# Local attention and feed-forward of a two-batch transformer: weights, tables and first rows loaded one stage earlier, shifted rows taken from transposed tokens

## What is computed

```python
def shift_token(t):               # second half of the channels from the token before
    t1, t2 = jnp.split(t, 2, axis=-1)
    t2 = jnp.pad(t2, ((0, 0), (1, 0), (0, 0)))[:, :-1]
    return jnp.concatenate([t1, t2], axis=-1)

def _layer(x, wqkv, qs, ksc, wo, lg, lb, w1, b1, w2, b2):
    q, k, v = jnp.split(shift_token(x) @ wqkv, 3, axis=-1)        # to 8 heads of 64
    q = l2norm(q) * qs
    k = l2norm(k) * ksc
    q, k = rotary_xpos(q, k)
    o = local_attention(q, k, v)  # windows of 128 tokens, each sees itself and the one before
    x = x + o @ wo
    h = shift_token(x)
    h = (h - mean(h)) / sqrt(var(h) + 1e-5) * lg + lb
    a, g = jnp.split(h @ w1 + b1, 2, axis=-1)                     # 2 x 682
    return x + (a * gelu(g)) @ w2 + b2
```

## Time and profile before

| | |
|---|---|
| median of 3 runs | 4666.85 us (4664.31 to 4668.85) |
| profiled execution, its own time | 4673.75 us |
| its span | 4672.1 us, mean granted TensorE clock 0.912 |
| TensorE / VectorE / ScalarE / GpSimd busy | 3969.5 / 2966.2 / 2041.8 / 670.3 us |
| output projection of the second attention, batch 0 | 1295.95 to 1321.80 |
| keeping the input | from 1322.99 |
| local attention, layer 0, batch 0 | from 1325.65 |
| feed-forward, layer 0, batch 0 | 1656.07 to 1827.97 |
| local attention, layer 1, batch 0 | from 1829.93 |

### The profile page before, as it was taken

How to read it: one execution, slowest core, us unless ns; L and a number is a source line. 1 busy time by engine, 2 the same in 40 slices (tenths; PEclk the granted TensorE clock), 3 DMA queues, 4 the chain that set the end, 5 groups by cost and what they waited for, 6 DMA issues and landing times. The chain is left out here.

```text
span 4672.1 us, 62196 instructions
## 1 busy us (share of the span) xinstructions
PE 3969.5 (85%) x21496; PEld 1945.2 (42%) x21588; DVE 2966.2 (63%) x5901; ACT 2041.8 (44%) x3649; POOL 670.3 (14%) x526
## 2 busy tenths in 40 slices
PE   7889967989969967996959899589899798779967
PEld 5233344333345534553533333433334354445534
DVE  3878765978657722773269786768785676237623
ACT  2356632456635511553124566215566454125521
POOL 2000004000023201331130000130000222023211
PEclk8799988899989988998978999789999899889989
DMA  3211002111010011001031110030110100110010
GB/s 82 32 29 28 2 2 48 28 29 28 2 46 8 4 36 45 8 7 29 9 73 28 29 29 2 20 50 9 29 28 2 47 8 11 30 45 8 5 33 23
DMA packets 149779, 117.45 MB, mean 25 GB/s; under 512 B 41192, under 2 KB 141008, under 8 KB 148944
## 3 DMA queue, kind: packets, MB, share of 16 engines
q1 hardware_dynamic: 142544, 107.20, 11.2%
q10 hardware_dynamic: 6912, 6.11, 0.4%
HBM read 41.15 MB, written 4.19 MB: 10 GB/s over the span
## 5 line engine op out<-in xcount | busy, mean ns | idle before, releaser
L735 DVE TENSOR_REDUCE chunk_max<-banks 128x1 f32<-128x512 f32 (+3 forms) x2240 | 1403.1, 669 | 218.2 <-PE banks L627 134.2
L702 ACT ACTIVATE probs<-banks 128x1024 f32<-128x1024 f32 (+3 forms) x1280 | 1084.2, 894 | 865.0 <-PE banks L671 435.8
L624 PE MATMUL banks<-stack_k,stack_q 96*128 96x512 bf16 (+3 forms) x2560 | 843.1, 376 | 138.5 <-DMA stack_k<-parts 54.9
L667 PE MATMUL banks<-stack_q,stack_k 99*128 99x512 bf16 (+3 forms) x2560 | 701.5, 351 | 7.4 <-ACT probs L702 7.4
L643 PE MATMUL banks<-probs,values_group 128*17 128x512 f32 (+3 forms) x5120 | 593.6, 536 | 0.0
L624 PEld LDWEIGHTS banks<-stack_k,stack_q 96*128 96x128 bf16 x2560 | 247.8, 100 | 788.3 <-DVE chunk_max L735 503.5
L1224 ACT ACTIVATE probs_l<-banks,nmax 128x256 f32<-128x256 f32 x512 | 238.2, 470 | 473.1 <-DVE nmax L1343 473.1
L1497 PE MATMUL banks<-hnT,w 128*128 128x512 f32 x768 | 354.6, 623 | 20.6 <-DVE hidden L1561 17.2
L1095 PE MATMUL banks<-wqkv,hT 128*128 128x512 f32 x768 | 362.5, 610 | 4.6 <-DMA wqkv<-in_L_ffn_wqkv 4.6
L1274 POOL TENSOR_TENSOR inv_norm<-ssum,mhalf 128x8 f32<-128x8 f32 x128 | 211.0, 1648 | 808.9 <-DVE ssum L1314 802.5
L667 PEld LDWEIGHTS banks<-stack_q,stack_k 99*128 99x128 bf16 x2560 | 241.2, 99 | 204.0 <-ACT probs L702 58.5
(11 more groups left out here) (182 smaller groups left out, 4810.9 us busy)
## 6 DMA issues: line engine op xcount, KB each, us to landing
stack_q<-parts SPq DMA_DIRECT2D x384, 64.0 KB, 2.4
stack_k<-parts SPq DMA_DIRECT2D x384, 64.0 KB, 2.4
xpos<-in_c_xpos SPq DMA_DIRECT2D x4, 1792.0 KB
wqkv<-in_L_ffn_wqkv SPq DMA_DIRECT2D x12, 512.0 KB, 9.4
w<-in_L_ffn_w ACTq DMA_DIRECT2D x16, 341.0 KB, 5.1
x_tok<-in_L_attn_x SPq DMA_DIRECT2D x8, 512.0 KB
rope<-in_c_rope SPq DMA_DIRECT2D x2, 2048.0 KB, 7.7
hs<-x_tok SPq DMA_DIRECT2D x64, 64.0 KB
```

Of the source, the lines that this page charges most:

```text
L624: ins = pe.matmul(out, sq[0:KS, c, j0 + j, i * P:(i + 1) * P], sk[0:KS, cc, j0 + j, 0:width], start=True, stop=not diag, skip_group_check= ...
L667: ins = pe.matmul(ps[:, SCORE + j, off:CH], keys, sq[0:KS + PARTS, c, j, off:CH], start=True, stop=not diag, skip_group_check=True)
L702: act.activation(probs[:, s % 2, 2 * half:2 * half + 2, off:CH], ps[:, SCORE + 2 * half:SCORE + 2 * half + 2, off:CH], ACT.Exp)\
L735: dve.tensor_reduce(chunk_max[:, n % 2, j:j + heads, i, cc], bank[:, 0:heads * width].rearrange("p (h n) -> p h n", h=heads), AX.X, ALU.ma ...
```

## The change

The second loop is unrolled in Python. `wqkv`, `wo`, the tables and the head scales live in a dict `local_weights` and are loaded by SP with `load_local_weights`: for layer 0 at the start of `project_out` of the second attention, for layer 1 in the feed-forward of layer 0 behind the last rows. The tables come whole (2 MB), and GpSimd multiplies them by the scales (`build_tables`) in these same two stages. The feed-forward's weights and vectors are loaded by SP at the start of the local attention of the same layer; its first rows follow there once four windows are added. Rows are loaded by four DMAs, the 127 partitions in parts of 112 and 15. In the local attention no rows are loaded: `turn_h` transposes `x` itself, `hT` is one column wider, the second half of the channels is read one column earlier, and its first column is copied from the window before. `keep_input` is gone; GpSimd copies a window at a time in the local attention of layer 0.

```diff
-            keep_input(k, keep)
-            with nc.Fori(0, DEPTH) as l:
-                local_attention(k, l, x2)
-                feed_forward(k, l, x2)
-            finish(k, b, keep)
+        F = ffn_weights(k, late)
+        for l in range(DEPTH):
+            local_attention(k, l, x2, F, keep)
+            feed_forward(k, l, x2, F)
+        finish(k, b, keep)
...
+            if layer:
+                @block.sync
+                def _(sp):
+                    load_local_weights(k, sp, 0)
+
+                @block.gpsimd
+                def _(pool):
+                    build_tables(k, pool)
...
+def load_local_weights(k, eng, l):
+    a, W, ahead = k["a"], k["local"], k["ahead"]
+    eng.dma_start(W["tab"][:, :, :, :], a["c_xpos"]).then_inc(ahead["tables"], 16)
+    for i in range(4):
+        w = a["L1_ffn_q_scale" if i < 2 else "L1_ffn_k_scale"]
+        for half in range(2):
+            s = (half + i) % 2
+            eng.dma_start(W["hscale"][:, i, half * 32:half * 32 + 32],
+                          w[l:l + 1, s * 32:s * 32 + 32].to_broadcast([P, 32])).then_inc(ahead["scales"], 16)
+    for i, done in enumerate(("w_q", "w_k", "w_v")):
+        own = slice(i * INNER, (i + 1) * INNER)
+        eng.dma_start(W["wqkv"][:, :, own], a["L1_ffn_wqkv"][l, :, own].rearrange("(t p) n -> p t n", p=P))\
+            .then_inc(ahead[done], 16)
+    eng.dma_start(W["wo"][:, :, :], a["L1_ffn_wo"][l].rearrange("(t p) n -> p t n", p=P)).then_inc(ahead["w_o"], 16)
+
+def build_tables(k, pool):
+    W, ahead = k["local"], k["ahead"]
+    pool.wait_ge(ahead["tables"], 16)
+    pool.wait_ge(ahead["scales"], 128)
+    for i in range(4):
+        t = W["tab"][:, i, :, :]
+        pool.tensor_tensor(t, t, W["hscale"][:, i:i + 1, :].to_broadcast([P, NT, LD]), ALU.mult)\
+            .then_inc(ahead["tab_ready"], 1)
...
+H_ROWS = 112
+
+def load_shifted(eng, hs, x2, c, done):
+    w = c * TPC
+    eng.dma_start(hs[:, :, 0:P], x2[:, w + 1:w + 1 + TPC, 0:P]).then_inc(done, 16)
+    for r0, r1 in ((0, H_ROWS), (H_ROWS, P - 1)):
+        eng.dma_start(hs[r0 + 1:r1 + 1, :, P:C], x2[r0:r1, w + 1:w + 1 + TPC, P:C]).then_inc(done, 16)
+    eng.dma_start(hs[0:1, :, P:C], x2[P - 1:P, w:w + TPC, P:C]).then_inc(done, 16)
...
@@ local_attention
-        hs, hT = sb("hs", [P, 2, C]), sb("hT", [P, 2, KT, P])
+        hT = sb("hT", [P, 2, KT, P + 1])
...
+                load_ffn_weights(k, sp, l, F)
+                sp.wait_ge(S["x_out"], TPC)
+                sp.wait_ge(S["masks"], 5)
+                load_shifted(sp, F["hs"], x2, 0, early["h_in"])
...
-                    pe.wait_ge(S[f"h{w % 2}"], 48 * (w // 2 + 1))
-                        ins = pe.transpose(ps[:, BH, t * P:(t + 1) * P], hs[:, w % 2, t * P:(t + 1) * P], identf[:, :])
+                        ins = pe.transpose(ps[:, BH, t * P:(t + 1) * P], x[:, w + 1, t * P:(t + 1) * P], identf[:, :])
...
-                        ins = pe.matmul(ps[:, bank, :], hT[:, w % 2, t, :], wqkv[:, t, i * INNER:(i + 1) * INNER],
+                        ins = pe.matmul(ps[:, bank, :], hT[:, w % 2, t, 1 - t:P + 1 - t], wqkv[:, t, i * INNER:(i + 1) * INNER],
...
-                    act.copy(hT[:, w % 2, :, :], ps[:, BH, 0:C].rearrange("p (t n) -> p t n", t=KT))\
+                    act.wait_ge(S["h_T_out"], 2 * w)
+                    act.copy(hT[:, w % 2, 1, 0:1], hT[:, (w - 1) % 2, 1, P:P + 1] if w else x[:, 0, 0:1])\
+                        .then_inc(S["h_T_out"], 1)
+                    act.copy(hT[:, w % 2, :, 1:P + 1], ps[:, BH, 0:C].rearrange("p (t n) -> p t n", t=KT))\
                         .then_inc(S["h_T_out"], 1)
...
+                if l == 0:
+                    zero_ffn_padding(k, pool, F)
...
+                    if l == 0 and w:
+                        pool.tensor_copy(keep[:, w - 1, :], x[:, w, :]).then_inc(S["kept"], 1)
...
-                make_tables(0, 0, EARLY)
+                dve.wait_ge(early["tab_ready"], 4)
...
-                make_tables(1, EARLY, NT)
@@ feed_forward
-                for c in range(NCH):
+                for c in range(1, NCH):
                     sp.wait_ge(S["normed"], TPC * c)
...
+                    load_shifted(sp, hs, x2, c, early["h_in"])
+                if l + 1 < DEPTH:
+                    load_local_weights(k, sp, l + 1)
...
                 loop(emit)(pool)
+                if l + 1 < DEPTH:
+                    build_tables(k, pool)
```

More of the change, by code:

```diff
@@ L129, in __getitem__, with end, scratch @@
         return self.by_name[name]
-    def end(self):
-        for s in self.by_name.values():
+    def end(self, also=()):
+        for s in [*self.by_name.values(), *also]:
             self.nc.sync.sem_clear(s)
         self.nc.all_engine_barrier()
-def scratch(k, ctx):
+def scratch(k, ctx, side=None):
     def sb(name, shape, dt=F32):
@@ L141, in sb @@
         n = k["names"].count(name)
-        return ctx.enter_context(k["nc"].sbuf_tensor(name if n == 1 else f"{name}_{n}", shape, dt))
+        return ctx.enter_context(k["nc"].sbuf_tensor(name if n == 1 else f"{name}_{n}", shape, dt, side=side))
     return sb
@@ L340, in quantise, with causal_attention @@
     assert count[0] == base + QUANT_STEPS
[L345 removed]
+def causal_attention(k, b, layer, late):
     with ExitStack() as ctx:
         sb = scratch(k, ctx)
[L348 removed]
         xT_o = sb("xT_then_o", [P, KT * T])
@@ new lines, in zero_ffn_padding, with load_ffn_weights @@
+def zero_ffn_padding(k, pool, F):
+    done = k["ahead"]["w_zero"]
+    pool.memset(F["w1"][:, :, :, HID:NHT * P], 0.0).then_inc(done, 1)
+    pool.memset(F["w2"][:, NHT - 1, :], 0.0).then_inc(done, 1)
+    pool.memset(F["b1"][:, :, :], 0.0).then_inc(done, 1)
+def load_ffn_weights(k, eng, l, F):
+    nc, a, ahead = k["nc"], k["a"], k["ahead"]
+    row = lambda w: w[l:l + 1, :]
+    n = HID - HLAST
+    eng.wait_ge(ahead["w_zero"], 3)
+    for i in (1, 0):
+        for t in range(KT):
+            eng.dma_start(F["w1"][:, t, i, 0:HID], a["L1_ffn_w1"][l, t * P:(t + 1) * P, i * HID:(i + 1) * HID])\
+                .then_inc(ahead["w1_in"], 16)
+    with nc.allow_non_contiguous_dma(reason="small vectors, one element to a partition"):
+        for i in range(2):
+            v = row(a["L1_ffn_b1"])
+            eng.dma_start(F["b1"][:, i, 0:NHT - 1], v[:, i * HID:i * HID + n].rearrange("o (t p) -> p (o t)", p=P))\
+                .then_inc(ahead["small_in"], 16)
+            eng.dma_start(F["b1"][0:HLAST, i, NHT - 1:NHT], v[:, i * HID + n:(i + 1) * HID]
+                          .rearrange("o (t p) -> p (o t)", t=1)).then_inc(ahead["small_in"], 16)
+        for dst, n_ in (("lg", "L1_ffn_ln_g"), ("lb", "L1_ffn_ln_b")):
+            eng.dma_start(F[dst][:, :], row(a[n_]).rearrange("o (t p) -> p (o t)", p=P)).then_inc(ahead["small_in"], 16)
+    eng.dma_start(F["b2"][:, :], row(a["L1_ffn_b2"]).to_broadcast([P, C])).then_inc(ahead["small_in"], 16)
+    eng.dma_start(F["w2"][:, 0:NHT - 1, :], a["L1_ffn_w2"][l, 0:n, :].rearrange("(t p) n -> p t n", p=P))\
+        .then_inc(ahead["w2_in"], 16)
+    eng.dma_start(F["w2"][0:HLAST, NHT - 1, :], a["L1_ffn_w2"][l, n:HID, :]).then_inc(ahead["w2_in"], 16)
@@ L1156, in _ @@
                 for i, come in enumerate(("w_q", "w_k", "w_v")):
-                    pe.wait_ge(S[come], 16)
+                    pe.wait_ge(early[come], 16)
                     project(0, i)
@@ L1385, in _, with feed_forward @@
                 add(NT - 1)
-    S.end()
-def feed_forward(k, l, x2):
+    S.end([early[name] for name in LOCAL_AHEAD])
+def feed_forward(k, l, x2, F):
     nc, a, ps, x, identf = k["nc"], k["a"], k["ps"], k["x"], k["identf"]
-    S = Stage(nc, k["pool"], "w2_in w1_0 w1_1 w_zero small_in h_in stats mv var rstd normed turned h_T ag gelued hidden y x_sum x_out")
+    S = Stage(nc, k["pool"], "halves stats mv var rstd normed turned h_T ag gelued hidden y x_sum x_out")
+    early = k["ahead"]
     BT, BA, BG, BY = 0, 2, 4, 6
@@ L1572, in _ @@
                 loop(emit)(dve)
-    S.end()
+    S.end([early[name] for name in FFN_AHEAD])
 def finish(k, b, keep):
```

172 lines of the change are left out of this document (53 added, 119 removed).

## The result

The changed kernel takes 4535.62 us (median of 4, 4534.39 to 4536.60), beside 4667.85 us for the kernel before in the same session: ratio 0.9713, 95% interval [0.9701, 0.9725], 132.2 us less. The forecast was 4540 in 4500 to 4585. The profiled execution's own time is 4535.16 us, its span 4533.5 us.

What follows compares the result with a forecast made beforehand. Bound by waits at stage starts, VectorE waiting 126.8 us for the feed-forward rows' DMA. Gains 173.6 less costs 46.2 take 127.4 us off 4673.75: 4546.4; the median being 6.9 lower, 4539.5, say 4540, range 4500 to 4585.

Steps and rivals of the forecast that it cites:

- feed-forward, first rows: Feed-forward start: chunk 0 loaded during local attention, statistics start about 0.3 us after T0; gain 21.6 x 4 = 86.4 us.
- feed-forward, chunk 1: Feed-forward: rows split into 112 and 15 partitions arrive in time, removing TensorE's stall and slow clock; gain 26.8 us.
- local, first rows: Local attention start: transposes need no DMA, first projection at T0 + 2.2 us; gain 51.5 us.
- (a): End of layer 0's feed-forward: GpSimd's four table multiplications stand with nothing over them; cost 18.8 us.
- (b): Second attention's output projection: GpSimd's table multiplications hold up VectorE; cost 12 us, bounds 0 and 18.8.
- (c): Layer 0: 16 GpSimd copies keeping the input prolong the hold on VectorE's scalings; cost 9 us at worst, 9 taken.
- (d): 64 one-column ScalarE copies, each ahead of the copy before the squares, 0.1 us each; cost 6.4 us, bounds 0 and 12.5.
- Rival D: Stage starts: TensorE keeps its full clock over the shorter gaps, saving 19 us more: 4521; chance 6 in 100.
- E: Feed-forward's first rows do not get in ahead, stuck in SP's queue behind weights; returns 86 us: 4626; chance 4 in 100.
- B: Feed-forward: the split load is still too slow and chunk 1's stall stays: 4567; chance 10 in 100.
- (f): Projections: stationary operands starting at odd elements load under the matmuls; costs nothing unless the load more than doubles.
- Rival F: Projections: slow stationary loads; 0.166 us wait per matmul cancels the gain, 0.25 us gives 4732; chance 4 in 100.

Runs made afterwards that it cites:

- e1: Changed kernel with the 127 partitions of every chunk's shifted rows loaded by one transfer again; 4561.13 us, ratio 0.9772 to the kernel before.
- e4: Changed kernel with the tables multiplied by VectorE inside local attention instead of by GpSimd; 4506.85 us, ratio 0.9654 to the kernel before.
- e10: Changed kernel with the shifted rows split into 126 and 1 partitions instead of 112 and 15; 4536.75 us, ratio 0.9717 to the kernel before.
- e5: Changed kernel with the input kept by one 2 MB transfer on SP's queue instead of sixteen GpSimd copies; 4533.02 us, ratio 0.9709 to the kernel before.
- e6: Changed kernel without ScalarE's 64 one-column copies, that part of the computation left out; 4533.62 us, ratio 0.9707 to the kernel before.
- e11: Changed kernel with the shifted rows split into 113 and 14 partitions instead of 112 and 15; 4556.31 us, ratio 0.9758 to the kernel before.
- e3: Kernel before with the loop over the two layers written out and nothing else; 4658.08 us, ratio 0.9976 to the kernel before.
- e9: Changed kernel with GpSimd's four table multiplications cut into sixteen of 128x256; 4534.88 us, ratio 0.9713 to the kernel before.
- e7: Changed kernel with both edits: tables multiplied by VectorE in local attention, input kept by one transfer; 4499.97 us, ratio 0.9636 to the kernel before.

## Why the prediction was right, point by point

Terms in microseconds over the program, both batches:

| step | predicted | measured | from |
|---|---|---|---|
| feed-forward, first rows | -86.4 | -85.0 | T0 to w1 matmul, 4 passes |
| feed-forward, chunk 1 | -26.8 | -30.5 | w1 matmul to last addition; e1 alone puts back 25.1 |
| local, first rows | -51.5 | -52.6 | T0 to projection, 4 passes |
| keep stage gone | -5.3 | -4.5 | output projection to T0, before less e4 |
| (a) tables after layer 0 | +18.8 | +18.4 | 10.76 less e4's 1.58, twice |
| (b) tables in the output projection | +12 | +10.3 | after less e4: 5.4 and 4.9 |
| first tables off VectorE's path | -3.6 | about -3.8 | first projection to first product, before and e10 at clock 0.74: 8.16 and 7.20, in 4 passes |
| (c) keep copies | +9 | +3.8 | e5, steady windows (by whole stages +4.4 to 5.0) |
| (d) one-column copies | +6.4 | +3.1 | e6, steady windows (by whole stages about +3.5) |

**Feed-forward and chunk 1.** Right in mechanism and size. The clock over the first w1 matmuls (1660.65 to 1665.40) is 0.51, the lower of TensorE's two levels, 1.2 GHz, as it was before (0.50 from 1685.76 to 1690.50), after 8 us in which TensorE did 1.94 us of transposes, so Rival D fell; at the first local attention it fell too, with a clock of 0.50 from 1330.36 to 1334.50. The rows are ahead, so E fell; no wait at chunk 1, so B fell, and e1 shows what B would have been: 4561, where it was put at 4567. By the rule of the Trainium skill cited at that step the 26.8 us would come in full; the ledger has 30.5, e1 alone 25.1, and e10, e11 and the engines' shares are the stricter test of it. Why the ledger has 5 us more than e1 is open.

**Local attention.** 1.75 us from T0 to the first projection, forecast 2.2: ScalarE's table load does not come first, it moved to the first exponential, where VectorE and ScalarE wait for scores anyway. Putting the 4 us of layer 1 to the loop's turn was right (e3).

**(a)** was exact. **(b)** was chosen between "one instruction at a time" (8.6) and "held throughout" (18.8), at 12; the mechanism is the first. VectorE gets in between two GpSimd instructions (e9: the holds shrink with the pieces), and three held instructions a stage make 5.4 and 4.9 us: in the rows of after they last 1.55, 1.77 and 2.1 us longer than their fellows. The Trainium skill's rule on a whole instruction ("SBUF — State Buffer", section "Who interferes with whom") is what these rows show. The mask copy of the earlier trace rows, which I read against it, ended with one memset in after's layer 1 (3.57 us beside one of 3.51) but outlasted one again in layer 0 (4.04 beside 3.52); what decides between the two is open. I leaned on one row where the rule was the better guide, at a price of 1.7 us.

**(c) and (d)** were mis-sized, in mechanism not refuted: both were taken near "every one of them is on the path". A keep copy costs 0.12 us, though it lasts 458 ns (mean of 32) and not the 300 that I took: a quarter of it is on the path. A column copy costs 0.05 us, half of what I took. A window grew by 0.05 us in layer 1 and 0.17 in layer 0, where 0.1 and 0.4 were forecast.

**(f), Rival F.** The stationary loads at odd elements, by-line groups of after against the earlier trace rows:

```profile
L1179 PEld LDWEIGHTS banks<-wqkv,hT 128*128 128x128 f32 x768 | 146.6, 198 | 158.8 <-issue 157.1
```

198 ns against 197: the shift costs nothing, and e6's windows of layer 1 (202.87 us for 202.86) leave nothing for it either.

**The sum.** In the profiled executions the program is 138.6 us shorter, where 127.4 were forecast. The measured terms of the table add up to 140.8 us, as do the totals of the ledger (1040.2 to 970.1 in the first batch, 1040.2 to 969.5 in the second); the rest of the program is 2.2 us longer. Against the forecast (c), (d), chunk 1 and (b) come to 13.9, and small terms take some back. Of the 11.2 between 138.6 and 127.4, 7 vanish again in the last step: before's profiled execution was 6.9 us above its median and I carried this over, but after's lies within 0.5 of its own. That 4540 is within 0.1% of 4535.6 is in part luck; the terms are less exact than their sum.

**Where the change left time.** It paid 28.7 us for the tables and some 4 for the copies that keep the input. Both are to be had: e7 takes 4499.97 us, 35.6 less than the changed kernel and 3.6% less than before.

## What to carry to other kernels

Look at the issue that stands behind a transfer: where it takes ten times its neighbours' time, change the partition count before anything is moved ahead; 113 and 127 were slow, 112 and 126 fast, and this alone gave 89 of 132 us. Work moved to an engine that seems free costs what it holds up: GpSimd's 9.2 us cost their full length at the end of a stage and half of it beside VectorE, while VectorE's own idle 5 us would have taken it for nothing. When several engines wait at a stage's start, ask for each row of the start which engine begins last; here the loop's turn held two queues that no busy time shows.

## What was not expected of the hardware

- A transfer of 113 partitions (226 KB) ran on about one DMA engine of 16 (share 0.07, 19 GB/s) and held the next issue on its queue 11 us; one of 126 (252 KB) ran on fourteen (0.87, 232 GB/s) and held it under 1 us.
- VectorE and GpSimd: single VectorE instructions of 0.16 to 0.41 us (the rows of 0.73, 1.64 and 2.83 us are two each) were stretched to 1.7 to 2.5 us by GpSimd instructions of 2.34 us and to 0.4 to 0.9 by ones of 0.72 us. One of the stretched ones was no large copy but a SCALAR_TENSOR_TENSOR of 4 columns that reads two SBUF tiles. Nothing that read PSUM was stretched.
- GpSimd's fixed cost: sixteen multiplications of 128x256 take 722 ns each (median) and four of 128x1024 2340 ns; 16 x 0.722 - 4 x 2.340 = 2.2 us for twelve instructions more, 0.18 us each.
- The turn of a hardware loop over two layers held SP's first issue 3.8 us behind the stage's T0 and ScalarE's first, of the scales, 2.9 us (1832.79 to T0 1829.93), while GpSimd's first instruction came 1.96 us after its last, against 1.6 to 2.1 without the loop.
